# GpSimd fills an unread row between two indirect transfers, in blocks 3 and 4 and for the first 14 outputs

## The reference

```python
# layer 0, expert_idx is one number per sample
h = gelu(einsum('bsh,bhi->bsi', x, Wi[expert_idx]) + bi)      # 128 -> 512
o = einsum('bsi,bih->bsh', h, Wo[expert_idx]) + bo            # 512 -> 128
y = layernorm(o + x) * gamma[expert_idx] + beta[expert_idx]
# layer 1
h = layernorm(y) * ln_g + ln_b
h = (h - h.mean(1)) * rsqrt(h.var(1) + 1e-8)                  # over the tokens of a sample
h = h * softplus(gamma_s) + beta_s                            # from a small network on the subject's id
gates, idx = top_k(softmax(h @ router_w), 2)                  # renormalised to sum 1
hid = relu(h @ exp_w1[e] + exp_b1[e]);  eout = hid @ exp_w2[e] + exp_b2[e]
out = y + sum over the two chosen e of gate * eout
```

## Time and profile before

| | us |
|---|---|
| median of 3 runs | 191.3 |
| lowest and highest | 190.03, 191.46 |
| the profiled execution | 191.05 |
| its span, first to last instruction | 189.3 |
| busy PE, DVE, ACT, POOL | 161.2, 130.4, 96.2, 112.4 |
| mean granted TensorE clock | 0.963 of full speed |

### The profile page before, as it was taken

How to read it: one execution, slowest core, us unless ns; L and a number is a source line. 1 busy time by engine, 2 the same in 40 slices (tenths; PEclk the granted TensorE clock), 3 DMA queues, 4 the chain that set the end, 5 groups by cost and what they waited for, 6 DMA issues and landing times.

```text
span 189.3 us, 5254 instructions
## 1 busy us (share of the span) xinstructions
PE 161.2 (85%) x1306; PEld 152.6 (81%) x1306; DVE 130.4 (69%) x636; ACT 96.2 (51%) x314; POOL 112.4 (59%) x170
## 2 busy tenths in 40 slices
PE   6699999699999998969999899999969999994000
PEld 5588898699999997968889799999959999993000
DVE  5624747998999899998997787853534555555073
ACT  3034935256675933966555927746544565651000
POOL 8950401437478798779848782777777645576000
PEclk9999999999999999999999999999999999999555
DMA  2999996279922458574646966776688874135494
GB/s 56 218 236 271 367 299 176 82 249 286 285 93 72 137 149 258 142 199 124 191 121 176 218 181 214 193 241 198 194 276 239 254 233 138 42 92 220 110 399 172
DMA packets 32478, 36.91 MB, mean 195 GB/s; under 512 B 4376, under 2 KB 21680, under 8 KB 32320
## 3 DMA queue, kind: packets, MB, share of 16 engines
q1 hardware_dynamic: 28816, 29.13, 55.4%
q0 software_dynamic: 3136, 7.40, 11.1%
q10 hardware_dynamic: 496, 0.04, 0.2%
HBM read 28.84 MB, written 7.71 MB: 193 GB/s over the span
## 4 chain that ended last, share of the span: by engine, by line
PE 30%; DVE 26%; DMA 14%; SPq 10%; issue 8%; POOL 7%; DVEq 3%; POOLq 0%
PE bank L1520 9%; PE bank L1535 9%; DMA pairs<-pair_rows 4%; PE bank L1328 4%; DMA pair_rows<-rows,slot 4%; POOL pair_rows L600 4%; SPq L408 3%; DVE st L801 3%; DVE x_w L768 3%; DMA hw<-in_L_cond_hyp_w_dram 3%; SPq L399 2%; SPq L367 2%; DMA o_all<-o_rows 2%; DVE mv L804 2%; DVE z L852 2%
## 5 line engine op out<-in xcount | busy, mean ns | idle before, releaser
L1225 ACT ACTIVATE hidden<-bank,b_c 128x128 f32<-128x128 f32 x156 | 44.4, 369 | 30.7 <-PE bank L1520 29.3
L605 POOL DMA_INDIRECT o_rows<-weighted,dest x39 | 37.6, 964 | 18.1 <-DVE weighted L967 11.9
L1535 PE MATMUL bank<-w_sb,hidden 128*128 x312 | 41.5, 277 | 0.8 <-DVE weighted L967 0.5
L1520 PE MATMUL bank<-h_t,win_w 128*128 128x128 f32 x312 | 41.5, 277 | 0.6 <-issue 0.3
L600 POOL DMA_INDIRECT pair_rows<-rows,slot x32 | 31.9, 997 | 15.7 <-issue 9.6
L1535 PEld LDWEIGHTS bank<-w_sb,hidden 128*128 128x128 f32 x312 | 37.8, 192 | 1.5 <-issue 1.5
L1520 PEld LDWEIGHTS bank<-h_t,win_w 128*128 128x128 f32 x312 | 37.9, 192 | 1.2 <-issue 0.5
L1165 ACT ACTIVATE hidden<-bank,bi_c 128x128 f32<-128x128 f32 x88 | 24.6, 373 | 14.8 <-PE bank L1422 14.7
L964 DVE TENSOR_TENSOR biased<-bank,b_all 128x128 f32<-128x128 f32 x39 | 11.3, 289 | 24.2 <-PE bank L1535 20.6
L1422 PE MATMUL bank<-x_t,win_w 128*128 (+1 forms) x176 | 23.1, 278 | 0.3 <-ACT x_t L1133 0.3
L1440 PE MATMUL bank<-wo_sb,hidden 128*128 x176 | 23.2, 275 | 0.0
(11 more groups left out here) (237 smaller groups left out, 242.1 us busy)
## 6 DMA issues: line engine op xcount, KB each, us to landing
win_w<-in_L_cond_exp_w_dram SPq DMA_DIRECT2D x39, 256.0 KB, 3.5
win_w<-in_L_cond_Wi_dram SPq DMA_DIRECT2D x22, 256.0 KB, 3.3
pairs<-pair_rows SPq DMA_DIRECT2D x39, 65.0 KB, 2.4
wo_sb<-in_L_cond_Wo_dram SPq DMA_DIRECT2D x8, 256.0 KB, 5.7
w_sb<-in_L_cond_exp_w_dram SPq DMA_DIRECT2D x8, 256.0 KB
o_all<-o_rows SPq DMA_DIRECT2D x4, 512.0 KB, 5.2
y_rows<-y SPq DMA_DIRECT2D x11, 128.0 KB
o_all<-in_x_dram SPq DMA_DIRECT2D x4, 256.0 KB, 5.3
```

What stands on the lines that cost most here:

```text
L605: pool.indirect_dma_start(o_rows, bass.IndirectOffsetOnAxis(dest[:, w:w + 1], 0), weighted[:, w % OUTS, :], None).then_inc(o_stored[w % OU ...
L1225: A.activation(hidden[:, w % 3, ft * P:(ft + 1) * P], bank[w % 2][:, ft * P:(ft + 1) * P], ACT.Relu, bias=b1_flat[:, bass.ds(bias, FT)][:, ...
L1520: last = mm(bank[w % 2][:, ft * P:(ft + 1) * P], win_w[:, (NW + w) % RING, ft * P:(ft + 1) * P], h_t[:, w % 3, :], start=True, stop=True)
L1535: last = mm(bank[3 + w % 2][:, 0:D], hidden[:, w % 3, ft * P:(ft + 1) * P], w2_sb[:, bass.ds(expert, FF)][:, ft * D:(ft + 1) * D], start=( ...
```

## The change

A helper `pause` fills the first partition of part_of_quarter (512 values) and waits for that fill. It is called ahead of every transfer of blocks 3 and 4 but each block's first, and at the start of store_out for windows 0 to 13, ahead of its wait.

```diff
+            def pause():
+                own.link(G_.memset(part_of_quarter[0:1], 0.0))
+
             def scatter(b, first, last):
                 for i in range(first, last):
+                    if b >= 3 and i:
+                        pause()
                     if i == 0:
                         pool.wait_ge(s["rows_numbered"], 2)
...
             def store_out(w):
+                if w < 14:
+                    pause()
                 pool.wait_ge(s["weighted_ready"], w + 1)
```

## The result

The changed kernel took 196.4 us (median of four, 195.8 to 198.8), the kernel before, beside it, 191.4: 2.8% slower, 95% interval 1.9 to 3.6%. The profiled execution took 195.8 us, its span is 194.0, so 4.7 more than before. The forecast was 196.9, with 5.65 us as the sum. On two other chips kernels close to this one came out faster than the kernel before; that is told with the experiments.

A forecast was written before the change was run, and what follows sets the result against it. GpSimd's transfers of blocks 3 and 4 were taken to set the end, through SyncE's loads of pairs and TensorE. The terms 4.0 − 1.2 + 2.85 = 5.65 us took the median from 191.3 to 196.9, range 193.5 to 199.0.

The forecast's parts named there:

- The price of a pause: On GpSimd, each pause replaces a gap of 0.30 by 0.02 + 0.53 + 0.25 and adds 0.07: 0.57 us.
- point 2: In scatter(3), seven pauses cost GpSimd 4.0 us; 1.2 us of slack before film(4) goes, TensorE's route(4) loses about 2.7.
- point 3: At load_pairs(13), block 3's pairs come 4.0 us later without further cost; SyncE reaches load_pairs(21) 4.0 late.
- point 4: At store_out(1) to (3), three pauses cost 1.7 us, barely hidden by the wait before scatter(4), with 0.6 left.
- point 5: From scatter(4), five unhidden pauses cost 2.85 us; SyncE waits about 3 us and load_pairs(21) is 5.65 late.
- point 6: From load_pairs(21) to load_pairs(25), SyncE's issuing and the landing shift whole, and TensorE behind them, by 5.65 us.
- point 7: At store_out(6) to (13), eight pauses cost 4.6 us, hidden: GpSimd is level again at window 32, ahead of gather_y.
- the dearer pause: Rival: each of the 12 pauses loses 0.24 us more to something shared; sum 8.5, so 199.8 us; chance 0.08.
- Faster, by relief of the DMA engines: Rival: spaced transfers let loads of pairs land in 1.8 us, gaining 2.25 us, so 189.05 us; chance 0.06.
- the cheaper pause (0.30): Rival: the next transfer starts 0.05 us behind the fill, so a pause costs 0.30 and the time is 193.7; chance 0.11.
- the free fill: Rival: filling one partition is nearly free, 0.13 us a pause, so 191.95 us, no measurable change; chance 0.07.
- theory 2: Formed after eight follow-up runs: on some chips dense trains of indirect transfers hold up DVE and ScalarE; pauses break the train.

The follow-up runs named there:

- no own wait: The changed kernel with the wait for each fill moved ahead of the next fill; 206.7 us against 216.2 for the kernel before, ratio 0.962, chip 9.
- the order of block 4 with pauses: The changed kernel, pauses kept, with scatter(4)'s last transfer moved ahead of store_out(4) and (5); 208.7 us, ratio 0.968 to the kernel before, chip 9.

## Why the prediction was right, and where not

- **The price of a pause**: 0.57 forecast, 0.495 measured. The fill (0.52) and the gap (0.28) were right within 0.03; the 0.07 added because a transfer behind a computation had taken 1.03 was wrong. Behind a fill a transfer takes 0.97. The 1.03 is seen again at 101.28 and 115.42, where a root is the last computation before the fill, with or without a wait for the fill (104.02 and 117.31 in the kernel without its own wait), so it seems to go with the root and not with the fill; why is open. This term alone makes 12 x 0.075 = 0.9 us, the size of the miss between 5.65 and 4.7.
- **Seven pauses, slack of 1.2** (point 2): scatter(3) to film(4) is 2.4 us longer than before (15.88 against 13.51), 2.8 forecast, so the slack was 1.2 as forecast (3.6 less 2.4). TensorE waited 1.94 us ahead of route(4), 2.7 forecast.
- **Block 3's arrival** (point 3): SyncE waited 4.2 us, and TensorE did not wait for these pairs.
- **The stores ahead of scatter(4)** (point 4): they just fitted in. The gap that remained was 0.56 us, 0.6 forecast; as two transfers with no wait between them stand 0.30 apart, the true wait was about 0.26.
- **Five pauses** (point 5): 2.51 us, 2.85 forecast. SyncE waited 2.9, "about 3" forecast.
- **The shift of the end** (point 6): from 124.95 to 129.37 it is 4.4 us; SyncE's issuing up to load_pairs(25) then took 0.57 less and that load's landing 0.86 more, which makes 4.7 at TensorE and at the end. The chain did not shift whole, as point 6 had it. The two groups alone add 2.24 up to scatter(4)'s start and 2.51 behind it, 4.75; scatter(3) had begun 0.33 us earlier (98.81 instead of 99.14). That the end shows 4.7 again is luck: 0.33 and 0.57 less are cancelled by the 0.86. TensorE waited 4.2 us in all for pairs between 112 and 150 us, 4.5 forecast for windows 21 to 25.
- **The eight hidden stores** (point 7): level with DVE at window 30, 165.09 us, ahead of gather_y; 32 forecast with the dearer pause.
- **The time**: the profiled execution took 195.8 us where 196.7 was forecast, so the 0.9 of the sum is missed there too. That the median of the four runs lies only 0.5 below the 196.9 is owed to the spread of the runs.
- **The rivals**: the cheaper pause (0.30), the free fill and the dearer pause are refuted by the pitch of 1.76. "Faster, by relief of the DMA engines" is wrong as a mechanism: on the chips where spacing makes the kernel faster, the DMA engines are three quarters idle during what it removes. Its outcome does occur there, with 3 to 4% in the kernels nearest to the change (no own wait, and the order of block 4 with pauses). The changed kernel as it is was not run on such a chip, so its own gain there stays open; an estimate is that its path costs about the same 4.7 us there, since the pitches are the same.

What was shown of theory 2: the stalls appear on chips 6 and 9, not on chip 4 nor in the first measurement, they follow the trains when these are moved, and they shrink with the pitch (long at 1.27 and 1.33, a remainder of 3.5 on ScalarE and 1.4 on DVE at 1.65, and at 1.76 none that begins in a paused stretch). Its mechanism was named wrongly: the waits were not fulfilled, and what comes late are TensorE's signals, up to 12.1 us.

What was not shown is why they come late, and why only TensorE's. The Trainium skill ("SBUF — State Buffer", section "Who interferes with whom") has a pair of ports shared by GpSimd and DVE, and gives ScalarE ports of its own. Such a pair would not stop ScalarE, which stopped for 6.8 us, nor delay a signal of TensorE, so the traces give it no support here. An untested rival is the recording itself: the traces with stalls lack 19 to 23% of the signals that their instructions raise, those without 1 to 2%, so on chips 6 and 9 records of signals were lost as well. Whether that is a cause or another result, no run here tells, since every run on record has a span and a clock of its own and none is known to have run unrecorded. Nor is it known what sets the two kinds of chip apart, or whether the same chip can change. Of all the kernels only the kernel before ran on both kinds, so no variant is known to be faster or slower on both.

## What to carry to other kernels

Price an inserted instruction by the start-to-start pitch of the queue, and then walk the queue to its next true wait: by the trace half of the pauses were free, because a wait or a later dense stretch swallowed them, and the same pauses up to window 33 cost about 9 us on top. Where the same kernel differs by 12% between chips, look at the stalls with no visible releaser first, and at the time at which the awaited semaphore was raised, before calling the waiting engine stalled. A change may gain on one chip and cost on another. Before a verdict on such a change, measure both kernels on more than one chip.

## What the runs showed of the hardware that was not expected

- On two chips TensorE's semaphores were raised up to 12.1 us behind their matmuls under a dense train of indirect transfers (1.27 to 1.33 us apart), so DVE stood for up to 11.2 us; the other engines' signals were on time. On a third chip 25 such transfers in a row did nothing of the kind (no signal more than 0.06 us late).
- A fill's price is the number of values in a partition: 1 x 512 values on one partition took 0.52 us and made the pitch 0.495 longer, a single value made it 0.06 longer. The wait for the engine's own semaphore adds 0.11 us (1.76 against 1.65).
- While TensorE stood in those stalls its granted clock fell to 0.50, and it still worked at that level at 148.43 (eight matmuls in 2.07 us instead of 1.06).
